# Graph network with row gathers: one gather in 27 replaced by single-row copies in every group, on two queues

## The reference, cut to what matters

```python
for l in range(3):
    xr = jnp.einsum('nd,rde->rne', x, W_rel[l])
    agg = segment_sum(xr[edge_type, src], dst, num_segments=6250)
    x = relu(agg + x @ W_root[l] + bias[l])
```

## Time and profile before

| | us |
|---|---|
| median of three runs | 5969.94 |
| lowest, highest | 5967.68, 5970.83 |
| the profiled execution's own span | 5964.9 |
| TensorE matmul busy | 4310.7 (72%) |
| TensorE weight load busy | 3901.4 (65%) |
| VectorE busy | 1844.7 (31%) |
| ScalarE busy | 619.0 (10%) |
| GpSimd busy | 4396.5 (74%) |

### The profile page before, as it was taken

One profiled execution on the slowest core, in us unless ns is written; L12 is line 12 of the kernel. 1 busy time (PEld: TensorE's weight loads), 2 busy tenths in 40 slices (PEclk: granted clock), 3 DMA queues, 4 the chain that ended last, 5 costly groups with the idle time before them and its releaser, 6 DMA issues.

```text
span 5964.9 us, 107654 instructions
## 1 busy us (share of the span) xinstructions
PE 4310.7 (72%) x26040; PEld 3901.4 (65%) x26041; DVE 1844.7 (31%) x3589; ACT 619.0 (10%) x848; POOL 4396.5 (74%) x4659
## 2 busy tenths in 40 slices
PE   4777777777777767777777777766776777776776
PEld 3666666666676656666666666666676666666666
DVE  5222222222222222222222222223333334333333
ACT  3001010010101000000000001000101011101111
POOL 5777777777777677777777777767777777777774
PEclk8898989898989888889999999888888888888887
DMA  6333333333333333333333333333333333333332
GB/s 196 113 111 113 112 112 112 111 114 111 113 112 112 107 111 110 111 111 111 110 111 111 111 110 112 110 106 113 114 113 115 113 113 114 114 113 114 113 113 74
DMA packets 296167, 674.77 MB, mean 113 GB/s; under 512 B 86202, under 2 KB 147387, under 8 KB 295772
## 3 DMA queue, kind: packets, MB, share of 16 engines
q0 software_dynamic: 222384, 607.55, 35.2%
q1 hardware_dynamic: 44686, 37.38, 2.1%
q10 hardware_dynamic: 28702, 26.46, 1.3%
HBM read 645.38 MB, written 25.68 MB: 112 GB/s over the span
## 4 chain that ended last, share of the span: by engine, by line
PE 27%; POOL 25%; issue 20%; SPq 15%; DMA 6%; DVEq 3%; DVE 3%; ACT 1%; ACTq 0%
POOL rows L403 25%; PE bank L421 15%; SPq L352 13%; PE bank L492 10%; DMA rows<-node_table,idx 5%; SPq L347 3%; DVE agg L1003 1%; ACT agg L708 1%; DVEq L986 1%; DVEq L989 1%; PE bank L618 1%; DVEq L1093 1%; PE bank L611 0%; DVE onehot L908 0%; PE bank L537 0%
## 5 line engine op out<-in xcount | busy, mean ns | idle before, releaser
L403 POOL DMA_INDIRECT rows<-node_table,idx x4633 | 4389.2, 947 | 1504.1 <-issue 1316.2
L421 PE MATMUL bank<-onehot,rows 128*128 128x128 f32 x18792 | 2700.1, 305 | 1422.5 <-DVE agg L1003 705.8
L421 PEld LDWEIGHTS bank<-onehot,rows 128*128 128x128 f32 x18792 | 2564.0, 218 | 1571.8 <-issue 1553.2
L1003 DVE TENSOR_TENSOR agg<-bank,agg 128x256 f32 x1566 | 663.7, 424 | 2079.8 <-PE bank L421 1575.6
L492 PE MATMUL bank<-wrel,agg 128*128 128x256 f32 x5568 | 1273.8, 388 | 44.4 <-DVE agg L1016 34.2
L492 PEld LDWEIGHTS bank<-wrel,agg 128*128 128x128 f32 x5568 | 1073.4, 195 | 200.0 <-issue 53.9
L908 DVE TENSOR_TENSOR onehot<-bank,key 128x1152 f32<-128x1152 f32 x525 | 707.0, 1347 | 0.0
L708 ACT COPY agg<-zero_col 128x2304 f32 x174 | 367.2, 2111 | 2928.9 <-PE bank L492 2928.9
L1025 DVE SCALAR_TENSOR_TENSOR acc<-bank,in_first,acc 128x256 f32 x174 | 84.2, 484 | 1777.6 <-PE bank L492 1680.9
L611 PE MATMUL bank<-wroot,nextT 128*128 128x256 f32 x392 | 146.7, 510 | 0.0
L715 ACT COPY acc<-bank 128x256 f32 (+1 forms) x98 | 36.5, 372 | 1004.7 <-PE bank L611 1004.7
(11 more groups left out here) (138 smaller groups left out, 800.1 us busy)
## 6 DMA issues: line engine op xcount, KB each, us to landing
far_rows<-node_table SPq DMA_DIRECT2D x7168, 1.0 KB
rows<-node_table,idx POOLq DMA_INDIRECT x4633
node_table<-new_x ACTq DMA_DIRECT2D x98, 128.0 KB
x_tile<-node_table SPq DMA_DIRECT2D x58, 128.0 KB, 2.2
x_in<-in_x_dram SPq DMA_DIRECT2D x8, 768.0 KB, 11.2
wrel<-in_L_gnn_W_rel_dram SPq DMA_DIRECT2D x6, 1024.0 KB, 8.2
xres<-in_x_dram ACTq DMA_DIRECT2D x48, 128.0 KB
out_dram<-res ACTq DMA_DIRECT2D x48, 128.0 KB
```

What stands on the lines that cost most here:

```text
L403: pool.indirect_dma_start(rows[:, s:s + D], None, tables[layer % 2], bass.IndirectOffsetOnAxis(ap=idx[:, g * TPG + k, j:j + 1], axis=0),). ...
L421: last = nc.tensor.matmul(to[:, h, :], of[:, s:s + P], hot[:, hot_k * CH + j, :], start=(j == 0), stop=(j == CH - 1))
L1003: nc.vector.tensor_tensor(window, seg[k % 3].rearrange("p h (r w) -> p h r w", r=R), window, ALU.add).then_inc(agg_added, 1)
```

## The change

- The last chunk of every group but the last (57 groups in each of the three layers, the constant `FETCHED`) comes row by row. GpSimd issues 26 gathers for such a group.
- SyncE issues rows 0 to 75 and ScalarE rows 76 to 127. There are two staging buffers (group parity), and TensorE reads them directly; VectorE's copy is gone.
- A row may be issued when VectorE has added everything of the group two before (a wait on `agg_added`).
- The node numbers are loaded as before, but laid over four partitions and turned once into byte addresses (shifted left by 10, on VectorE). The table is viewed as bytes.
- In layer 0 SyncE issues its 76 rows of a group before the node tile of that group.
- ScalarE issues its rows for the next group in two parts: 20 rows before it takes over the next node sums (or before the sign of the outcome in the last layer), 32 rows behind that and before it zeroes `agg`. For this the LNS part of `ended` is split in three.
- SyncE issues the weights of the next layer before it waits for the last stores.
- In the path for groups that are spread over more tiles (not taken with sorted edges as given here) a copy and a flattened loop replace the nested loop.

```diff
-FETCHED = GROUPS // 2 - 1
-HALF = P // 2
+FETCHED = GROUPS - 1
 LOADS = 32
+QUARTERS = P // LOADS
+SP_ROWS = 76
+ACT_ROWS = P - SP_ROWS
+SP_HALF = SP_ROWS // 2
+ROW_BYTES = D * 4
...
+    table_bytes = [t.rearrange("n d -> (n d)").bitcast(u8).unsqueeze(0) for t in tables]
...
+        far_at = at("far_at", [QUARTERS, FETCHED * LOADS], i32, edges_at)
-        far_rows = sb("far_rows", [P, D], fp32)
+        far_rows = sb("far_rows", [P, 2 * D], fp32)
...
+        def far_row(p, b):
+            return far_rows[p:p + 1, b * D:(b + 1) * D].bitcast(u8)
+        def far_from(layer, at_byte):
+            return table_bytes[layer % 2][:, ds(at_byte, ROW_BYTES)]
+        def far_starts(engine, g, q, first, end):
+            _, starts = nc.values_load_multi_w_load_instructions(
+                far_at[q:q + 1, ds(g * LOADS + first, end - first)], engines=[engine], min_val=0, max_val=(N - 1) * ROW_BYTES,
...
+            return starts
...
+            def fetch(layer, g, b):
+                if not isinstance(g, int):
+                    sp.wait_ge(agg_added, g * TPG + (layer * TRIPLES + 3 - TPG))
+                    sp.sem_inc(sp_mark, 1)
+                for q in range(QUARTERS - 1):
+                    first, end = q * LOADS, min(SP_ROWS, (q + 1) * LOADS)
+                    for p, start in zip(range(first, end), far_starts(SP, g, q, 0, end - first)):
+                        sp.dma_start(far_row(p, b), far_from(layer, start)).then_inc(far_by_sp[layer][b][p // SP_HALF], 16)
+            load_tile(0, 0)
+            sp.wait_ge(far_at_ready, 1)
+            fetch(0, 0, 0)
+            with sp.Fori(0, (TILES - 1) // 2) as i:
+                fetch(0, i * 2 + 1, 1)
+                load_tile(i * 2 + 1, i * 2 + 1)
+                fetch(0, i * 2 + 2, 0)
+                load_tile(i * 2 + 2, i * 2 + 2)
...
+            for layer in range(1, L):
+                sp.wait_ge(out_ready, layer * GROUPS)
+                load_weights(layer)
+                sp.wait_ge(stored, 16 * TILES * layer + 16)
+                fetch(layer, 0, 0)
+                with sp.Fori(0, FETCHED // 2) as i:
+                    fetch(layer, i * 2 + 1, 1)
+                    fetch(layer, i * 2 + 2, 0)
...
-                        for j in range(CH - 1 if layer and g % 2 and k == TPG - 1 else CH):
+                        for j in range(CH - 1 if k == TPG - 1 else CH):
...
+                        row = of[:, s:s + P]
+                        if far is not None and j == CH - 1:
+                            row = far_rows[:, far * D + h * P:far * D + (h + 1) * P]
...
+            def far_landed(layer, g, b):
+                pe.wait_ge(gathered[TPG - 1], g * (16 * (CH - 1)) + (layer * FETCHED + 1) * (16 * (CH - 1)))
+                for h in range(2):
+                    pe.wait_ge(far_by_sp[layer][b][h], g * (8 * SP_HALF) + (2 - b) * 8 * SP_HALF)
+                pe.wait_ge(far_by_act[layer][b], g * (8 * ACT_ROWS) + (2 - b) * 8 * ACT_ROWS)
...
+            def fetch_quarter(layer, g, b, q, first):
+                for m, start in enumerate(far_starts(SCALAR, g, q, first, LOADS)):
+                    act.dma_start(far_row(q * LOADS + first + m, b), far_from(layer, start)).then_inc(far_by_act[layer][b], 16)
+            def fetch_first(layer, g, b):
+                if not isinstance(g, int):
+                    act.wait_ge(agg_added, g * TPG + (layer * TRIPLES + 3 - TPG))
+                    act.sem_inc(act_mark, 1)
+                fetch_quarter(layer, g, b, QUARTERS - 2, SP_ROWS % LOADS)
+            def fetch_second(layer, g, b):
+                fetch_quarter(layer, g, b, QUARTERS - 1, 0)
+            def fetch_ahead(layer, g, part):
+                with act.If(g < FETCHED - 1):
...
+                    with act.If(g % 2 > 0):
+                        part(layer, ahead, 0)
+                    with act.Else():
+                        part(layer, ahead, 1)
...
-                if late and layer < L - 1:
+                if late and layer == L - 1:
                     with act.If(g < late[0]):
-                        next_sums(layer, late[1])
+                        turned_tile(late[1])
+                fetch_ahead(layer, g, fetch_first)
+                if late:
+                    with act.If(g < late[0]):
+                        if layer < L - 1:
+                            next_sums(layer, late[1])
+                        else:
+                            out_of_tile(late[1])
+                fetch_ahead(layer, g, fetch_second)
                 act.wait_ge(out_ready, gg + 1)
...
-            def take_fetched(layer, g):
...
-                nc.vector.tensor_copy(rows[:, s:s + D], far_rows[:, :]).then_inc(far_copied, 2)
```

More of the change, by code:

```diff
@@ L32 @@
 XCHUNKS = 8
-FETCHED = GROUPS // 2 - 1
-HALF = P // 2
+FETCHED = GROUPS - 1
 LOADS = 32
+QUARTERS = P // LOADS
[3 more added lines that the diff above has]
+ROW_BYTES = D * 4
+ROW_SHIFT = 10
+NINTH, NINTH_SHIFT = 57, 9
+assert all((j * NINTH) >> NINTH_SHIFT == j // TPG for j in range(TILES * TPG))
 LN_EPS = 1e-5
@@ L414, in _, with products @@
             pe.reg_mov(owed, 0)
-            def products(to, of, hot, k=0, hot_k=0):
+            def products(to, of, hot, k=0, hot_k=0, far=None):
                 for h in range(KH):
@@ L445, in rows_of @@
+            def rows_of(layer, g, k, b=None):
+                if k < TPG - 1:
+                    pe.wait_ge(gathered[k], (g + layer * GROUPS) * (16 * CH) + 16 * CH)
+                elif b == 0:
+                    far_landed(layer, g, 0)
+                else:
+                    with pe.If(g < FETCHED):
+                        far_landed(layer, g, 1)
                         pe.sem_inc(pe_mark, 1)
@@ L451, in extra_products @@
                     pe.reg_mov(owed, 0)
-                    for k in range(TPG):
+                    for k in range(TPG - 1):
                         rows_of(layer, g, k)
+                    with pe.If(g % 2 > 0):
+                        rows_of(layer, g, TPG - 1, 1)
+                    with pe.Else():
+                        rows_of(layer, g, TPG - 1, 0)
+                        pe.sem_inc(pe_mark, 1)
                     pe.wait_ge(rel_loaded, 32 * (layer + 1))
@@ L692, in _ @@
             act.wait_ge(ends_loaded, 16)
+            act.wait_ge(far_at_ready, 1)
+            def fetch_quarter(layer, g, b, q, first):
[10 more added lines that the diff above has]
+                with act.If(g < FETCHED - 1):
+                    ahead = nc.s_assert_within(g + 1, 1, FETCHED - 1, skip_runtime_bounds_check_because="the branch is taken in front of the last fetched group")
+                    with act.If(g % 2 > 0):
+                        part(layer, ahead, 0)
+                    with act.Else():
+                        part(layer, ahead, 1)
+                    act.sem_inc(act_mark, 1)
             def group(layer, g, late=None):
@@ L788, in _ @@
                     next_sums(layer, TILES - 1)
+                else:
+                    turned_tile(TILES - 1)
+                    out_of_tile(TILES - 1, last=True)
             act.wait_ge(x_res_loaded, 16 * TILES)
@@ L813, in _ @@
             dve.sem_inc(agg_ready, 1)
-            dve.sem_inc(far_copied, 2)
             def statistics(c):
```

148 lines of the change are left out of this document (68 added, 80 removed).

## The result

The changed kernel takes 6105.15 us (median of 4 runs, 6100.88 to 6107.6), the kernel before beside it 5969.73 us: a ratio of 1.0227, 95% interval 1.0212 to 1.0241. It is slower by 2.3%, where 0.4% faster was forecast.

What follows compares the result with a forecast made beforehand. The gathers were taken as the bound, in the last layer beside the loop of VectorE, TensorE and ScalarE. Layer terms of −6 − 36 + 20 = −22 us on 5969.9 gave 5948 us, range 5875 to 6105.

Steps and rivals of the forecast that it cites:

- What goes: Layer 0 loses 57 gathers, layers 1 and 2 lose 29 each: 71, 36 and 36 us at 1.251 us.
- SyncE's row: On SyncE, byte addresses remove the multiply, so a row takes 0.342 us instead of 0.423.
- SyncE's return: SyncE's loop pauses 2.8 us on returning, once per two groups, 1.4 us per group.
- Layer 0: SyncE's turn of 33.3 us per group sets layer 0, which ends at 2026 against 2031.6: 6 us gained.
- The rival with no pause on SyncE: SyncE's loop returns without pausing, gathers bound layer 0, ending at 1963; 5885 us in all, chance 0.2.
- Layer 2: ScalarE's rows lie on the last layer's loop: 20 us lost instead of 36 gained.
- ScalarE's return: In layer 2, the loop's own steps and the ends of four new branches add about 0.7 us.
- the chain of 35.2 us: In layer 2, ScalarE's work from one root to the next takes 35.2 us, against 34.1 before.
- the slower rival: ScalarE's loop pauses 2.5 us per return: last-layer groups of 37.7 us, 144 us lost there, 6072 in all; chance 0.3.

Runs made afterwards that it cites:

- e5: The changed kernel with SyncE's and ScalarE's loops moved by never-executed blocks (48 and 64 instructions on SyncE); 5889.3 us.
- e6: e5 plus GpSimd gathering the last chunk of the very first group, SyncE and ScalarE starting with group 1; 5880.68 us.
- e1: The changed kernel with loops moved only, by never-executed instructions: 66 and 58 on SyncE, 60 on ScalarE; 5919.07 us.
- e16: The changed kernel with only ScalarE's loops moved, by 60 never-executed instructions in front of layer 1; 5963.56 us.
- e3: e2 with 76 more never-executed instructions in front of the last layer; 5973.13 us, ratio 1.0001 to the kernel before.
- e2: The kernel before with 90 and 130 never-executed instructions in ScalarE's loop over tiles of the last layer; 5975.15 us.
- e4: The changed kernel with ScalarE's 52 rows of the last layer in four pieces where it waits; 5997.94 us.
- e7: e6 plus ScalarE's rows of the last layer in four pieces in its waits, as in e4; 5823.7 us.
- e8: e7 plus ScalarE, instead of SyncE, issuing the node tiles of layer 0; 5823.09 us.
- e17: The changed kernel with only SyncE's loops moved, by two never-executed blocks of 48 and 64 instructions; 6033.86 us.

## Why the prediction was wrong, step by step

- **What goes** was right. 1506 gathers per layer; layer 1 gained 38 us for 36.
- **SyncE's row** was right in kind and slightly too dear: no multiply, and 0.326 us from row to row on average (0.342 computed; ScalarE's 0.336). A turn with its node tile takes 31.4 us for 31.9.
- **SyncE's return** was argued from the loop's size ("about 400, so this row is near"), and size does not decide. In layers 1 and 2 the loop didn't pause (0.24 us), which changed nothing, since the gathers bound layer 1. In layer 0 it stopped twice.
- **Layer 0** failed in that term: 2.8 us per two groups, 1.4 per group, was a fair reading of the earlier trace rows, but the two stops are 5.2 us. The layer lost 22 us where it should have gained 6, 28 in all. Over the whole layer a group of SyncE's took 33.65 us for 33.3, 20 us in 56 groups (34.0 in the long loop, less behind it); the first row was issued at 88.2 us instead of 83.6; and one more pause, 3 us, stood in front of the last node tile. The rival with no pause on SyncE gave 1963 for the end of layer 0; e5 shows 1974. That e6 shows 1963.0 is partly luck, since it has another edit at the start.
- **Layer 2** is where the prediction failed most, +156 us for +20, in the term of ScalarE's return: "The loop's own steps and the ends of four branches that were not there add about 0.7", which held no pause; the pause measured 3.1 us. The rest of the chain of 35.2 us was right, since without the pause (e1, e16) the groups with a tile take 34.9 to 35.1 us from root to root and the layer is 13 to 17 us longer than before, for 20 computed. With the pause the slower rival applied, as written: ScalarE's loop pauses, "layers 0 and 1 hide it, but in the last layer" it counts. Its 2.5 us were 3.1, its 37.7 us 38.4, its 144 us 156; its total of 6072 lacks these and layer 0. It had 0.3 where the forecast had 0.4, and it was the case. Its "layers 0 and 1 hide it" was half luck: in layer 0 there was no pause to hide.
- What I didn't see in the earlier trace rows is the slack. ScalarE's 5.90 us in front of the root was idle time that the 52 rows used up: from root to the end of the zeroing lie 28.3 us before (median) and 35.0 after. e3 shows that a pause of 3 us would have been free before. The rows made the queue the bound, and only that gave the pause a price, 48 groups × about 3 us.
- The range did not hold either: it ended at 6105, just under the median, and the chances put slower (0.41) below faster (0.47).
- The rule of the Trainium skill ("Runtime: NRT & Kernel Launch", instruction fetch mechanics), that a taken branch out of a window of two pages, 32 KB in all, waits for a fetch, was rightly put behind the rival: that the place of a loop decides is what the runs show. With pages of that size, 256 instructions each, the trace disagrees. SyncE's loop of 332 pauses where it stands in the changed kernel and 69 instructions further on (e1), and doesn't pause 51 further on (e5). Two such pages would hold it where it starts on one of the first 181 places of a page, and no starting place gives all three outcomes.

## What to carry to other kernels

Before rows, loads or branches are put into a queue's loop, look at how far its program reaches and at the idle time in front of its first waiting instruction: once that idle time is spent, a loop return of 3 us is paid on every turn. When a loop pauses on return, move it by a block of code that never runs before giving up the edit; here that alone turned a loss of 2.3% into a gain of 0.9%, and with both queues right 1.4%. Work that is issued by a queue belongs where that queue waits anyway.

## What the runs showed of the hardware that was not expected

Whether a loop pauses depends on its position in steps of 128 instructions. The trace shows fetches in packets of 8.19 KB (5.96 MB in 728); the Trainium skill ("Perfetto Trace Analysis", the 4-stage model) has 64 bytes to an instruction, which makes 128 to a packet, by an estimate from the two. The table counts the instructions of each queue's compiled program in order, without the markers of branch targets, which no trace shows as executed, and fits one origin per queue, the same in all kernels. The expectations were written with a rougher count, by which ScalarE's loops had 282, 307, 295 and 331 instructions instead of 274, 296, 288 and 315.

```
loop (instructions)                      starts at, of 128   stretches   return, us
SyncE layer 0, changed (332)                   127               4       2.95, then 2.27
SyncE layer 0, e1 (332)                         68               4       2.96
SyncE layer 0, e5 (332)                         50               3       0.23
SyncE layer 0 end, changed / e1 / e5 (328)  76 / 17 / 127     4 / 3 / 4  3.0 / 0.22 / 3.2, then 2.06
SyncE layers 1 and 2, changed (322)          52 and 20           3       0.24
ScalarE layer 0, changed (274)                   2               3       0.20
ScalarE layer 1, changed (274)                 121               4       2.91
ScalarE layer 2, changed / e1 (296)         108 / 43           4 / 3     3.11 / 0.23
ScalarE layer 2, e2 / e3 (288)               46 / 124          3 / 4     0.22 / 2.97
ScalarE layer 2, e4 / e7 (315)              108 / 46           4 / 3     2.63 / 0.21
ScalarE layer 2, loop inside, e4 (281)         116               4       2.82
ScalarE layer 2, loop inside, changed (262)    116               3       0.21
```

Every loop that reaches over four such stretches pauses and none that keeps to three does, in these rows and in all other loops of SyncE and ScalarE in the kernel before, the changed one, e1 to e8, e16 and e17; two loops of 274 instructions in one program, 9 positions apart within a stretch, differ by 2.7 us. The loops that stop a second time, one instruction behind the branch, all start on one and the same place of a stretch, also in e6 and e7 (2.79 then 2.34 us, 2.67 then 2.13), and no other loop starts there. The origins are fitted: for SyncE 39 to 48 fit the pauses, and the table takes 48, which makes that place the last of a stretch; for ScalarE 64 to 69 fit, and it takes 66. So the four stretches are an inference; the positions of ScalarE's loops in e1, e2, e3 and e7 were set by it beforehand, and it held each time, with some luck, as the count was 7 to 16 instructions off in the loops' lengths.

A smaller one: two queues that issue rows at the same time don't slow each other's issuing. The DMA instruction of a row took 225 ns on SyncE (median), as in the kernel before where ScalarE issued none, and 232 ns on ScalarE; 32 registers take 2.02 to 2.15 us on either.
